# Attention mask written by ScalarE instead of TensorE, and scores moved behind a projection, in a six-layer stack

## The reference, cut to what matters

```python
def local_attention(q, k, v):            # w = 32, nw = 512 / 32
    ...
    mask = (it < jb) | (it > jb + w) | (jb == -1)
    sim = jnp.einsum('bhwie,bhwje->bhwij', bq, bk2) * QK_SCALE
    sim = jnp.where(mask, -jnp.finfo(sim.dtype).max, sim)
    attn = jax.nn.softmax(sim, -1)
    out = jnp.einsum('bhwij,bhwje->bhwie', attn, bv2)
...
for i in range(DEPTH):                   # 6
    x = attn_layer(shift_tokens(x), Wqkv[i], q_scale[i], k_scale[i], Wo[i]) + x
    x = ffn_layer(shift_tokens(x), ln_g[i], ln_b[i], W1[i], b1[i], W2[i], b2[i]) + x
```

## Time and profile before

| | |
|---|---|
| median of 3 runs | 2013.47 us (2012.26 to 2022.57) |
| the profiled execution, its own time | 2011.62 us |
| its span | 2009.8 us |
| the stack in it | about 596 to 1530 us |
| PE, DVE, ACT, POOL busy over the span | 83%, 64%, 44%, 32% |
| PE busy from 1100 to 1200 us | 95.04 of 100 us |

### The profile page before, as it was taken

How to read it: one execution, slowest core, us unless ns; L and a number is a source line. 1 busy time by engine, 2 the same in 40 slices (tenths; PEclk the granted TensorE clock), 3 DMA queues, 4 the chain that set the end, 5 groups by cost and what they waited for, 6 DMA issues and landing times.

```text
span 2009.8 us, 42786 instructions
## 1 busy us (share of the span) xinstructions
PE 1660.6 (83%) x17607; PEld 1119.5 (56%) x17607; DVE 1281.4 (64%) x2378; ACT 883.5 (44%) x1640; POOL 637.3 (32%) x994
## 2 busy tenths in 40 slices
PE   3005277799777999899998999999987999999999
PEld 1002155477544656556656656656654677777676
DVE  5845775412757878688887888887863555555311
ACT  1033033223234656456555656556544455445332
POOL 0000021100227756656756656756740000000000
PEclk6556588799888999999999999999998999999999
DMA  3000002010023533342432443433311000000111
GB/s 93 20 4 12 3 0 60 11 32 24 0 78 94 139 101 99 93 104 80 126 101 75 128 104 87 121 100 94 87 40 43 1 1 1 1 1 1 32 32 32
DMA packets 73806, 113.40 MB, mean 56 GB/s; under 512 B 16086, under 2 KB 36156, under 8 KB 73582
## 3 DMA queue, kind: packets, MB, share of 16 engines
q1 hardware_dynamic: 72798, 110.43, 20.0%
q10 hardware_dynamic: 816, 0.24, 0.1%
HBM read 83.98 MB, written 27.50 MB: 55 GB/s over the span
## 4 chain that ended last, share of the span: by engine, by line
PE 61%; DVE 27%; ACT 5%; issue 5%; DMA 1%; DVEq 1%; ACTq 0%; POOL 0%; SPq 0%; POOLq 0%
PE PS L1343 7%; PE PS L1071 6%; PE PS L1062 6%; PE PS L2029 4%; PE PS L1532 4%; PE PS L1976 3%; PE PS L1998 3%; PE PS L1580 3%; PE PS L1446 3%; DVE st_t L1386 2%; DVE st_ss L1391 2%; DVE st_r L1378 2%; DVE al_hist L455 1%; PE PS L1472 1%; PE PS L1512 1%
## 5 line engine op out<-in xcount | busy, mean ns | idle before, releaser
L1419 POOL TENSOR_TENSOR st_r<-st_r,st_t 128x512 f32<-128x512 f32 x192 | 243.5, 1272 | 252.5 <-DVE st_t L1386 252.5
L1343 PE MATMUL PS<-st_wqkv,st_xs 128*128 128x512 f32 x576 | 302.0, 609 | 16.4 <-DVE st_xs L1593 9.9
L1434 POOL TENSOR_TENSOR st_r<-st_r,st_gy 128x512 f32<-128x512 f32 x192 | 196.6, 1055 | 3.8
L1378 DVE TENSOR_TENSOR st_r<-PS,st_rot 128x512 f32<-128x512 f32 x192 | 129.9, 676 | 90.1 <-ACT st_sqh L1362 89.8
L2091 ACT ACTIVATE la_p<-PS,la_nmx 128x589 f32<-128x589 f32 x128 | 95.1, 748 | 133.4 <-DVE la_nmx L2122 133.4
L2122 DVE TENSOR_REDUCE la_nmx<-PS 128x1 f32<-128x589 f32 x128 | 92.7, 766 | 91.6 <-PE PS L1984 91.6
L1362 ACT ACTIVATE st_sqh<-PS 128x512 f32<-128x512 f32 x192 | 114.3, 595 | 57.5 <-PE PS L1343 57.5
L1130 ACT ACTIVATE m_h<-PS 128x512 f32<-128x512 f32 x128 | 76.2, 598 | 141.4 <-PE PS L1062 141.3
L1155 DVE SCALAR_TENSOR_TENSOR m_y<-PS,m_g,m_y 128x128 f32<-128x128 f32 x112 | 31.5, 344 | 161.2 <-PE PS L1071 161.2
L1386 DVE TENSOR_TENSOR st_t<-PS,st_rot 128x512 f32<-128x512 f32 x192 | 130.7, 680 | 0.0
L1071 PEld LDWEIGHTS PS<-m_w,m_h 128*128 128x128 f32 x1024 | 121.6, 196 | 16.0 <-issue 16.0
(11 more groups left out here) (316 smaller groups left out, 3501.0 us busy)
## 6 DMA issues: line engine op xcount, KB each, us to landing
st_v_out<-st_v SPq DMA_DIRECT2D x48, 512.0 KB, 2.6
st_vv<-st_v_out SPq DMA_DIRECT2D x96, 256.0 KB, 4.0
st_vv<-st_v_out SPq DMA_DIRECT2D x96, 192.0 KB, 4.7
st_wqkv<-in_st_wqkv SPq DMA_DIRECT2D x18, 512.0 KB, 5.8
m_w<-in_m_w SPq DMA_DIRECT2D x32, 256.0 KB, 3.0
st_vv<-st_v_out SPq DMA_DIRECT2D x72, 64.0 KB, 1.9
st_wo<-in_st_wo SPq DMA_DIRECT2D x6, 512.0 KB
st_w<-in_st_w SPq DMA_DIRECT2D x6, 341.0 KB
```

The source lines that it names most:

```text
L1343: pe.matmul(PS[:, 2 + m % 2, :], self.xs[:, b, P * t:P * t + P], self.wqkv[:, l % 2, k, 512 * half:512 * half + 512], start=True, stop=Tru ...
L1378: dve.tensor_tensor(h3(self.r[:, t % 2, c, :]), h3(ps), self.rot[:, k, 0, t, :].unsqueeze(1) .broadcast_to([P, 8, D2]), ALU.mult)
L1419: pool.tensor_tensor(r, r, self.t2[:, c % 2, :], ALU.add).then_inc(self.added, 1)
L1434: pool.tensor_tensor(r, r, y[:, 8 * c:8 * c + 8].unsqueeze(2).broadcast_to([P, 8, D2]), ALU.mult)\
```

## The change

ACT writes the mask into banks 0 and 1 as one copy of 1024 columns (`act_mask`), at the end of the step before, and a new semaphore `masked` tells PE. The two mask matmuls and the identity's load go. `pe_scores` now follows the first projection of the step. The 32 matmuls of `pe_mix` set the start flag only on the first of each bank and row of tiles, and at step -1 PE writes banks 0 and 1 once with `centre`, ahead of the first mask.

```diff
@@ pe_scores
             pe.wait_ge(self.r_evac, 4 * T + 4)
-            if T > 0:
-                pe.wait_ge(self.on_ready, T)
-            for e in range(2):
-                pe.matmul(PS[:, e, :], self.identb[:, :],
-                          self.wmask[:, min(t, 1), :].unsqueeze(1).broadcast_to([P, 8, 2 * WIN]),
-                          start=True, stop=False, skip_group_check=True)
+            pe.wait_ge(self.masked, T + 2)
@@ new function
+        def act_mask(self, act, T):
+            t = T % self.TILES
+            if T == 0:
+                act.wait_ge(self.c_in, 32)
+                act.wait_ge(self.masked, 1)
+            else:
+                act.wait_ge(self.on_ready, T)
+            act.activation(PS[:, 0:2, :].rearrange("p e (c k) -> p (e c) k", c=8),
+                           self.wmask[:, min(t, 1), :].unsqueeze(1).broadcast_to([P, 16, 2 * WIN]), ACT.Copy)\
+               .then_inc(self.masked, 1)
@@ pe_mix
-                                   ..., start=True, stop=True,
+                                   ..., start=(c % 4 == 0), stop=(c % 4 == 3),
@@ pe
-                if here:
-                    self.pe_scores(pe, T)
+                if T == -1:
+                    for e in range(2):
+                        mm = pe.matmul(PS[:, e, :], const("centre"), self.xs[:, 0, :], start=True, stop=True)
+                    mm.then_inc(self.masked, 1)
                 if past:
                     self.pe_turn_o(pe, T - 1, 0)
                 if lead:
                     self.pe_proj(pe, T + 2, 0)
+                if here:
+                    self.pe_scores(pe, T)
                 if past:
                     self.pe_turn_o(pe, T - 1, 1)
@@ act, at the end of a step
                 if lead:
                     self.act_proj(act, T + 2, 5)
+                if turn:
+                    self.act_mask(act, T + 1)
```

More of the change, by code:

```diff
@@ L1189, in __init__ @@
             self.wmask = s("wmask", [P, 2, 2 * WIN], BF16)
-            self.identb = s("identb", [P, P], BF16)
             self.xs = s("xs", [P, B, S])
@@ L1224, in __init__ @@
              self.rstd, self.spread, self.ln_tmp, self.ffn_in, self.up, self.gelu, self.act_ready, self.down,
-             self.down_added, self.scaled) = [
+             self.down_added, self.scaled, self.masked) = [
                 sem("st_" + what) for what in (
@@ L1229, in __init__ @@
                 "sub_done exps den_ready rden_ready v_stored pv_done on_ready wo_done xu_ready xf_ready centred lnsq "
-                "var std rstd spread ln_tmp ffn_in up gelu act_ready down down_added scaled").split()]
+                "var std rstd spread ln_tmp ffn_in up gelu act_ready down down_added scaled masked").split()]
             self.vshift = [sem("st_vshift%d" % t) for t in range(4)]
@@ L1300, in sp @@
             sp.dma_start(self.wmask[:, :, :], io["st_wmask"]).then_inc(self.c_in, 16)
-            sp.dma_start(self.identb[:, :], io["identb"]).then_inc(self.c_in, 16)
             for k in (2, 0, 1):
@@ L1532, in pe_mix @@
                     mm = pe.matmul(PS[g, c // 4, P * (c % 4):P * (c % 4) + P], self.pT[:, c, g],
-                                   self.vv[:, 4 * (T % 2) + w, :, D2 * c:D2 * c + D2], start=True, stop=True,
+                                   self.vv[:, 4 * (T % 2) + w, :, D2 * c:D2 * c + D2], start=(c % 4 == 0), stop=(c % 4 == 3),
                                    tile_position=(0, WIN * w), skip_group_check=True)
@@ L1692, in pe @@
         def pe(self, pe):
-            pe.wait_ge(self.c_in, 48)
             pe.wait_ge(self.set_up, 5)
```

## The result

The changed kernel takes 2034.26 us (median of 4 runs, 2027.94 to 2039.96), the kernel before 2017.21 us beside it: ratio 1.0069, interval 1.0038 to 1.0101. A second measurement of the unchanged file, ten runs of it, gave 2037.13 against 2020.63 us: 1.0076 (1.0053 to 1.0099), which is 15 us (11 to 20). So it is slower. The forecast of 2035 us hits the time almost exactly, but that is partly luck: it rests on a run of 2011.62 us, and the median of the kernel before rose from 2013 to 2017 and 2021 us with more runs. The forecast's ratio was 2034.7 / 2011.62 = 1.0115, which is above both intervals. The direction and the mechanism were right, the size was some 8 us too large.

The account below looks back on a forecast made before the run. No engine was taken to bound the kernel alone; the chain passes between PE and DVE. From 2011.62 us, +14.1 (late scores) +11.6 (clock) -1.1 (t = 0) -1 (start) -0.5 (end) gave 2034.7 us; range 2018 to 2044.

Parts of the forecast that it names:

- t = 2: Step where PE waits for `xs`: scores moved behind the projection make `pe_wo` 1.41 us late, ten times, +14.1 us.
- clock drops: Behind the 2.5 us standstill PE's clock falls: seven of ten times at 1.65 us each, +11.6 us.
- Rival 1: The clock holds: scores late by 1.41 us ten times, no drop follows; 2023 us, chance 0.20.
- t = 0: Step bound by PE, 11 times: saved mask time mostly spent waiting for ACT's mask; gain 0.1 us each, -1.1 us.
- t = 1: Step 11 times: `pe_wo` gains 0.4 us, but the chain goes over DVE; value 0.
- t = 3: Step that is DVE's from end to end; value 0.
- The start: Start of the stack: added `centre` matmuls fall into PE's 3.66 us wait for POOL, clock may hold; -1 us.
- Rival 2: Faster: moved scores cost nothing and 19 mask pairs on the chain come back; 2001.5 us, chance 0.07.
- Rival 3: No change: the 1.41 us disappears in DVE's waits; 2009 to 2013 us, chance 0.10.
- rival 4: ACT's mask takes 1.5 us or more, t = 0 and t = 1 lose 0.4 us each, 22 times; 2044, chance 0.05.

Follow-up runs that it names:

- filler: The changed kernel with two unread 512-column matmuls in front of the first projection at t = 2; 2027.54 us, 1.0029 of the kernel before.
- split_order: The changed kernel with the scores kept at the head of the step at t = 2 only; 2025.57 us, 1.0015 of the kernel before.
- changed_again: The changed kernel as it is, timed again in five rounds; 2037.13 us, 1.0076 of the kernel before.
- move_only: The kernel before with only the mask matmuls and scores moved behind the first projection, no mask on ACT; 2044.02 us, 1.0122 of the kernel before.
- changed_tables_early: The changed kernel with DVE's table build moved ahead of the maximum at t = 2; 2038.48 us, 1.0089 of the kernel before.

## Why the prediction was right, and where its size was off

**The wait at t = 2 held exactly.** Idle time of 2.53 us ten times, `xs` no earlier, scores behind the projection, `pe_wo` late by the scores' length. I priced this at 1.41 us each; with a full clock and no tables it is 1.50 us (41.97 - 40.47), and `filler` shows it without the clock. `split_order` shows no cost of anything else in the change that could be told.

**The count of clock drops came out nearly as forecast, their price lower.** Seven drops forecast, eight seen. I took 1.65 us for each. A drop lengthens the two steps by 1.1 to 1.2 us (43.09 and 43.19 against 41.97), by 0.7 us where there are tables (about 43.4 against the 42.70 of `filler`), and by 2.0 us in the one at 0.50. That is 8 to 9 us for the eight instead of 11.6, and `filler` gives 8 to 9 us back. The likely reason is that part of the slow stretch lies where PE is not alone on the chain; that is argued, not shown. Rival 1, the clock that holds, is out: gaps of 2.53 us dropped it eight times in ten, and 32 times in 40 over the four traces that have them (`changed_again`, `move_only` and `changed_tables_early` are the others). The rule of the Trainium skill that I set beside it ("TensorE: Matmul & The Clock Gate", section "Why this matters for your kernels"), which warns only of longer gaps, does not hold here; the measurement decides.

**The step that failed** is the one that priced every t = 2 alike: "Price: 10 x 1.41 = 14.1 us". In five of the ten, DVE's table build followed, and the lateness freed it of POOL: 3.15 us became 1.43 us (1.96 us where the clock holds). Five times 1.2 us, 6 us in all, came back by the later scores alone, and up to 8 us where the clock had dropped as well. My text followed the chain "from the `xs` copy" to the rotation and took from a step without tables that what lies behind only shifts. I did not ask of DVE's work what runs beside it on POOL. This is the greater part of the 8 us by which the sum was too large. The clock's price adds 3 us to it, and t = 0 and the price of a late score take 2 and 1 us off again.

**t = 0, t = 1, t = 3.** The mask copy takes 1.02 us, not 1.06, and `pe_wo` comes 0.12 us sooner at t = 0, as forecast; but the step becomes 0.06 us longer, not 0.1 us shorter. The forecast credited `pe_wo`'s lead to the time without asking who waits for it there; where the 0.06 us come from was not traced. PE's pause for the mask at t = 0 is 1226.64 - 1226.28 = 0.36 us, shorter than the 0.5 us I gave. t = 1 is unchanged at 17.54 us, as forecast.

**The start** came out at 1 us by luck. I had the `centre` matmuls fall into PE's wait for POOL and keep the clock up behind it. They ran some 4 us before it began, the wait stayed at 3.66 us and the transposes at 2.12 us. The 0.98 us lie ahead of the stack: its first projection starts at 595.35 us instead of 596.39, and from there to the first subtraction both kernels take 29.5 us. Over the twelve traces that first start scatters from 595.35 to 598.09 us, with both ends in kernels that have the change.

**The rivals.** Rival 2 wanted the 10 us of mask pairs on the chain back. They were replaced by a wait for ACT at t = 0, and `split_order` bounds their worth at 2 us. Rival 3 is excluded by the interval, and rival 4 by 1.02 us.

## What to carry to other kernels

Before an instruction is moved behind a wait, ask if it could have run inside that wait; work that an engine did while it had to wait anyway is free, and taking it out can cost twice: its length behind the wait, and the clock that its absence drops. When a delay is followed along a chain, look at each link for what another engine does beside it: a shift of one or two microseconds changed DVE instructions by a factor of two to three here, in both directions. And weigh busy time taken from the busiest engine by the chain alone: 25 us off PE brought no gain that could be told.

## What the runs showed of the hardware

- An equal standstill of PE, 2.53 us, drops the granted clock to 0.50 to 0.70 over the next 5 us in eight cases of the changed kernel's trace and leaves it at 1.00 in two; over four traces it is 32 drops in 40. With 1.9 us of work put in and 0.82 us left idle it never dropped in ten.
- DVE copies of 512 columns on 64 partitions to `xf` take 0.42 us alone and 1.18 to 1.27 us in the step shown, beside POOL's 512-column products. Four table products with two SBUF inputs take 1.43 us alone and 3.15 us beside them.
- An ACT copy of 1024 bf16 columns into two fp32 banks takes 1.02 us.
- PE shows idle gaps of up to 4.5 us that end with no event, eight to thirteen in a trace and 17 to 32 us in all. All 133 stand at the same place in a count of 256 PE rows. What ends them was not tested, and they limit how well single executions of such a kernel can be compared.
